# Last rope group's parts in buffers of their own, made and moved eight tiles later; VectorE casts tiles 3, 5 and 7 of a batch

## What is computed

```python
c_kv = x @ w_dkv
c_q = x @ w_dq
k_r = _apply_rope((x @ w_kr).reshape(b, s, 1, DR), cos, sin)
k_n = (c_kv @ w_uk).reshape(b, s, HKV, DN)
q_r = _apply_rope((c_q @ w_qr).reshape(b, s, H, DR), cos, sin)
q_n = (c_q @ w_uq).reshape(b, s, H, DN)
q = jnp.concatenate([q_r, q_n], axis=-1)
v = (c_kv @ w_uv).reshape(b, s, HKV, DV)
scores = jnp.einsum('bqhd,bkhd->bhqk', q, k) * scale
attn = jax.nn.softmax(scores, axis=-1)
out = jnp.einsum('bhqk,bkhd->bqhd', attn, v)
```

## Time and profile before

| | |
|---|---|
| median of 3 runs | 903.22 us (901.86 to 906.53) |
| the profiled execution | 900.48 us, its span 898.7 us |
| TensorE matmul, busy share | 96% |
| ScalarE | 76% |
| VectorE | 75% |
| GpSimd | 69% |

### The profile page before, as it was taken

How to read it: one execution, slowest core, us unless ns; L and a number is a source line. 1 busy time by engine, 2 the same in 40 slices (tenths; PEclk the granted TensorE clock), 3 DMA queues, 4 the chain that set the end, 5 groups by cost and what they waited for, 6 DMA issues and landing times.

```text
span 898.7 us, 16917 instructions
## 1 busy us (share of the span) xinstructions
PE 860.2 (96%) x5128; PEld 498.8 (56%) x5128; DVE 675.0 (75%) x1063; ACT 682.0 (76%) x1111; POOL 616.5 (69%) x438
## 2 busy tenths in 40 slices
PE   8999789999999999999999978999999999999995
PEld 5568344445444454458786733445444454446874
DVE  1879987888888888863577987888888888884455
ACT  2744789999999999971453489999999999995142
POOL 0318867888878888881344786788878887786135
PEclk8999999999999999999999999999999999999998
DMA  9865999999898899996201699999899999998101
GB/s 243 236 241 119 181 205 176 173 196 173 162 193 169 169 186 174 168 179 217 94 24 36 153 191 194 179 178 191 163 175 187 169 171 191 172 174 181 61 1 48
DMA packets 423964, 145.82 MB, mean 162 GB/s; under 512 B 408220, under 2 KB 416240, under 8 KB 423152
## 3 DMA queue, kind: packets, MB, share of 16 engines
q1 hardware_dynamic: 423152, 142.91, 78.2%
q0 software_dynamic: 608, 2.10, 0.7%
q10 hardware_dynamic: 160, 0.26, 0.1%
HBM read 23.85 MB, written 7.60 MB: 35 GB/s over the span
## 4 chain that ended last, share of the span: by engine, by line
PE 71%; DVE 8%; SPq 5%; ACT 4%; POOL 4%; issue 4%; DMA 4%; DVEq 0%; ACTq 0%; POOLq 0%
PE Tb L1269 18%; PE OO L1240 13%; PE Sa L1240 12%; PE Sb L1240 8%; PE Ta L1251 5%; PE Sa L1387 3%; PE Sb L1387 2%; SPq L369 2%; SPq L338 2%; DMA PT_dma<-P_parts 1%; PE Sb L1279 1%; ACT probs L633 1%; POOL turned L442 1%; DVE QO L1023 1%; PE OO L1129 1%
## 5 line engine op out<-in xcount | busy, mean ns | idle before, releaser
L468 POOL TENSOR_TENSOR P_parts<-probs,P_parts 128x768 f16<-128x768 f32 x256 | 419.9, 1658 | 106.5 <-ACT P_parts L526 106.4
L526 ACT ACTIVATE P_parts<-probs 128x768 f16<-128x768 f32 x256 | 205.6, 842 | 6.5 <-DMA PT_dma<-P_parts 5.2
L926 DVE TENSOR_TENSOR PT_lo<-Ta,PT_hi 128x512 f16<-128x512 f32 x128 | 88.5, 691 | 62.5 <-ACT PT_hi L526 60.0
L902 DVE TENSOR_REDUCE small<-OO 128x1 f32<-128x1024 f32 x96 | 117.1, 1220 | 21.4 <-PE OO L1240 21.4
L1269 PE MATMUL Tb<-PT_dma,V_hi 128*64 128x512 f16 x768 | 132.1, 385 | 0.0
L633 ACT ACTIVATE probs<-OO,small,scales 128x1024 f32<-128x1024 f32 x96 | 115.4, 1202 | 18.3 <-DVE small L905 16.7
L1240 PE MATMUL OO<-K_hi,Q_parts 128*128 128x512 f16 x384 | 115.5, 383 | 10.1 <-ACT probs L633 8.3
L902 DVE TENSOR_REDUCE small<-Sa 128x1 f32<-128x1024 f32 x96 | 116.9, 1217 | 8.4 <-PE Sa L1240 8.4
L1240 PE MATMUL Sa<-K_hi,Q_parts 128*128 128x512 f16 x384 | 115.9, 384 | 3.6 <-ACT probs L633 3.6
L633 ACT ACTIVATE probs<-Sa,small,scales 128x1024 f32<-128x1024 f32 x96 | 115.6, 1204 | 4.9 <-DVE small L905 2.5
L902 DVE TENSOR_REDUCE small<-Sb 128x1 f32<-128x1024 f32 x64 | 77.9, 1218 | 12.1 <-PE Sb L1240 12.1
(11 more groups left out here) (303 smaller groups left out, 1551.7 us busy)
## 6 DMA issues: line engine op xcount, KB each, us to landing
Q_parts<-turned_parts SPq DMA_DIRECT2D x64, 128.0 KB, 2.4
TT<-ternary SPq DMA_DIRECT2D x2, 2304.0 KB, 8.4
Q_parts<-Q_parts SPq DMA_DIRECT2D x16, 256.0 KB, 3.1
PT_dma<-P_parts SPq DMA_TRANSPOSE x256, 3.9
ternary<-tern SPq DMA_DIRECT2D x1, 2304.0 KB, 9.9
wo<-in_L_attn_w_o_dram SPq DMA_DIRECT2D x4, 512.0 KB, 9.7
xq<-in_L_attn_x_dram SPq DMA_DIRECT2D x2, 1024.0 KB, 10.6
wq_low<-Wq_lo SPq DMA_DIRECT2D x1, 2048.0 KB, 14.3
```

Of the source, the lines that this page charges most:

```text
L468: nc.gpsimd.tensor_tensor(P_parts[:, n % DEEP, 1, :], probs[n % DEEP][:, KP * P:S], P_parts[:, n % DEEP, 0, :], ALU.subtract).then_inc(par ...
L526: return nc.scalar.activation(o, i, ACT.Copy, scale=scale)
L902: nc.vector.tensor_reduce(nmax[:, n % 4:n % 4 + 1], scores_bank(n)[:, :], AX.X, ALU.max, negate=True).then_inc(row_max, 1)
L926: nc.vector.tensor_tensor(PT_lo[place].rearrange("p k (t q) -> p t k q", t=2), T_BANK[:, :].rearrange("p (t k q) -> p t k q", t=2, k=KP), ...
```

## The change

- The rotated halves of group 3 go to a buffer `turned_end` and their parts to `parts_end`. Both lie where `Wq_lo` was. So GpSimd's two sums of group 3 now wait until all query products are done (`q_ps`), and no longer for the low parts of group 2.
- VectorE makes the parts of group 3 in the steps n = 8 and n = 12 of pair 0, not in n = 0 and n = 2.
- SyncE issues group 3's latent moves ahead of tiles 9 and 10, and its rotary moves ahead of tiles 13 and 15. Before it prefetches `Wvo_lo` and `xr` (which lie where the new buffers are) it waits for those moves.
- The 768-column cast of tiles 3, 5 and 7 of each batch is done by VectorE (`odd_high`), directly behind `PT_lo`. GpSimd then waits for `odd_hi`.
- TensorE's wait for group 3 stands at the end of each of the pairs 1 to 6, not of pair 0.

```diff
+ODD = (3, 5, 7)
...
+        (turned_end, parts_end), AT = lay(
+            K_AT - H * 2 * P * 4, ("turned_end", [P, 2, S], F), ("parts_end", [P, 2, 2, S], F16))
...
-                        if first and n in (3, 5):
+                        if first and n == 8:
+                            for j in range(2):
+                                sp.wait_ge(turned_out[j], (b + 1) * 64 * GROUPS - 64)
+                        if first and n in (9, 10):
+                            t = 4 * (GROUPS - 1) + 2 * (n - 9)
+                            sp.wait_ge(lat_lo, (b + 1) * 4 * GROUPS)
+                            sp.dma_start(Q_parts[64:128, t, :, :], Q_parts[0:64, t + 1, :, :]).then_inc(lat_moved, 16)
+                        if first and n in (13, 15):
                             sp.wait_ge(lat_moved, (b + 1) * 32 * GROUPS)
-                            rotary_moves(GROUPS - 1, n // 2 - 1)
-                        if first and n == 8:
-                            sp.wait_ge(lat_moved, (b + 1) * 32 * GROUPS)
-                            for j in range(2):
-                                sp.wait_ge(turned_out[j], (b + 1) * 64 * GROUPS)
+                            rotary_moves(GROUPS - 1, n // 2 - 6)
...
+                for j in range(2):
+                    sp.wait_ge(turned_out[j], (b + 1) * 64 * GROUPS)
...
-                        if g >= 1:
+                        if g == GROUPS - 1:
+                            pool.wait_ge(q_ps, (b + 1) * 4 * GROUPS)
+                        elif g >= 1:
                             pool.wait_ge(rope_lo[j], b * GROUPS + g)
...
+                    if odd:
+                        pool.wait_ge(odd_hi, b * len(ODD) + ODD.index(n) + 1)
+                        pool.sem_inc(part_hi, 1)
+                    else:
+                        hold(pool, part_hi, tile + 1)
...
+                            if not (first and n + 3 in ODD):
+                                cast(n + 3)
...
+                def odd_high(tile, n):
+                    dve.wait_ge(exp_done, EXP0 + tile + 1)
+                    if n >= DEEP:
+                        dve.wait_ge(part_in[n % DEEP], 16 * (tile // DEEP))
+                    nc.vector.tensor_copy(P_parts[:, n % DEEP, 0, :], probs[n % DEEP][:, KP * P:S]).then_inc(odd_hi, 1)
...
-                        if first and n in (0, 2):
-                            rotary_parts_high(GROUPS - 1, n // 2)
+                        if first and n in (8, 12):
+                            rotary_parts_high(GROUPS - 1, n // 4 - 2)
                         transposed_low(pair * (TILES // 2) + n // 2, n + 1)
-                        if first and n in (0, 2):
-                            rotary_parts_low(GROUPS - 1, n // 2)
+                        if first and n in (8, 12):
+                            last_parts_low(n // 4 - 2)
+                        if first and n + 3 in ODD:
+                            odd_high(t0 + n + 3, n + 3)
...
-                        if first and n == TILES - 2:
+                        if not (first or last) and n == TILES - 2:
                             pe.wait_ge(lat_moved, b * 32 * GROUPS + 32 * GROUPS)
```

More of the change, by code:

```diff
@@ L96, in build @@
             K_AT - H * 2 * P * 4, ("Wvo_lo", [P, PAIRS, D], R), ("xr", [P, QT, D], F))
+        assert AT <= K_AT
+        (turned_end, parts_end), AT = lay(
+            K_AT - H * 2 * P * 4, ("turned_end", [P, 2, S], F), ("parts_end", [P, 2, 2, S], F16))
         assert AT <= K_AT
@@ L243, in build @@
         pt_ps, pt_hi, pt_lo = sem("pt_ps"), sem("pt_hi"), sem("pt_lo")
-        part_hi, part_lo = sem("part_hi"), sem("part_lo")
+        part_hi, part_lo, odd_hi = sem("part_hi"), sem("part_lo"), sem("odd_hi")
         part_in = tuple(sem(f"part_in{i}") for i in range(DEEP))
@@ L335, in rotary_moves @@
                 def rotary_moves(g, j):
+                    parts = parts_end if g == GROUPS - 1 else turned_parts
                     sp.wait_ge(rope_lo[j], b * GROUPS + g + 1)
@@ L338, in rotary_moves @@
                         sp.dma_start(Q_parts[32 * j:32 * j + 32, 4 * g + s, :, :],
-                                     turned_parts[32 * s:32 * s + 32, j, :, :]).then_inc(turned_out[j], 16)
+                                     parts[32 * s:32 * s + 32, j, :, :]).then_inc(turned_out[j], 16)
                 for g in range(GROUPS):
@@ L345, in _ @@
                         t = 4 * g + 2 * i
-                        sp.wait_ge(lat_lo, b * 4 * GROUPS + 4 * g + 2 * i + 2)
-                        sp.dma_start(Q_parts[64:128, t, :, :], Q_parts[0:64, t + 1, :, :]).then_inc(lat_moved, 16)
+                        if g < GROUPS - 1:
+                            sp.wait_ge(lat_lo, b * 4 * GROUPS + 4 * g + 2 * i + 2)
+                            sp.dma_start(Q_parts[64:128, t, :, :], Q_parts[0:64, t + 1, :, :]).then_inc(lat_moved, 16)
                     if g < GROUPS - 1:
@@ L463, in low_out, with low_probs @@
                                             O_parts[:, pair_row, cols].bitcast(F), ALU.subtract).then_inc(out_lo, 1)
-                def low_probs(tile, n):
-                    hold(pool, part_hi, tile + 1)
+                def low_probs(tile, n, odd=False):
+                    if odd:
[3 more added lines that the diff above has]
+                        hold(pool, part_hi, tile + 1)
                     nc.gpsimd.tensor_tensor(P_parts[:, n % DEEP, 1, :], probs[n % DEEP][:, KP * P:S],
@@ L474, in pair_pool @@
                         h = n // 8
-                        low_probs(pair * TILES + n, n)
+                        low_probs(pair * TILES + n, n, first and n in ODD)
                         if n % 8 == 0 and not (first and h == 0):
@@ L681, in pair_act @@
                         if ahead and behind:
-                            cast(n + 3)
+                            if not (first and n + 3 in ODD):
+                                cast(n + 3)
                 part_high(b * PAIRS * TILES, 0, None)
@@ L918, in rotary_parts_high, with last_parts_low @@
                     dve.wait_ge(rope_sum, b * 2 * GROUPS + 2 * g + j + 1)
-                    dve.wait_ge(turned_out[j], b * 64 * GROUPS + 64 * g)
-                    nc.vector.tensor_copy(turned_parts[:, j, 0, :], turned[:, j, :]).then_inc(rope_hi, 1)
+                    nc.vector.tensor_copy(parts_end[:, j, 0, :], turned_end[:, j, :]).then_inc(rope_hi, 1)
+                def last_parts_low(j):
+                    dve.wait_ge(rope_hi, (b + 1) * 2 * GROUPS - 1 + j)
+                    nc.vector.tensor_tensor(parts_end[:, j, 1, :], turned_end[:, j, :], parts_end[:, j, 0, :],
+                                            ALU.subtract).then_inc(rope_lo[j], 1)
                 def transposed_low(tile2, n):
```

3 lines of the change are left out of this document (2 added, 1 removed).

## The result

The changed kernel takes 910.09 us (median of 12 runs, 907.14 to 913.4), the kernel before 902.73 us (median of 12 runs beside it). The ratio is 1.0088 (95% interval 1.0071 to 1.0105): slower by about 0.9%. The forecast of 904.8, its range to 908.2 and its likeliest case, no measurable change, were all wrong. The two medians differ by 7.4 us, where 1.6 were forecast.

What follows compares the result with a forecast made beforehand. TensorE was taken to bound settled attention, a VectorE-ScalarE chain the first half of pair 0. Losses of 1.2 us (batch 1) and 0.4 (batch 0), +1.6 on the median 903.22, gave 904.8 us; range 898.8 to 908.2.

Steps and rivals of the forecast that it cites:

- The chain without group 3: First half of pair 0: VectorE-ScalarE chain of 4.43 us a step, tile 9's exponential 2.4 us earlier in batch 1.
- The piece in n = 8: Pair 0, one half of group 3's parts on VectorE: step of 6.83 us, leaving 0.4 of the 2.4 us gained.
- The piece in n = 12: Pair 0, other half of group 3's parts: step of 7.2 us, tile 17's exponential 1.9 us late in batch 1.
- VectorE's share: Pair 0, TensorE's loss after both pieces: 1.2 us in batch 1 and 0.4 in batch 0, +1.6 us.
- The sum's term for SyncE: End of pair 0: later moves delay tile 16's DMA 4 us, tile 20's cast waits; counted 0, bound 1 us a batch.
- Rival 2: TensorE's clock falls after idling before tile 15: 1.6 us lost a batch, 908.0 us in all; chance 0.11.
- Rival 3: VectorE's new casts of tiles 5 and 7 each wait 1.1 us for GpSimd: 909.2 us in all; chance 0.07.
- Rival 1: Group 3's pieces in n = 8 and 12 miss GpSimd, each step costing 1.9 us: 898.4 us in all; chance 0.25.
- TensorE's wait in the loop: Hardware loop: wait finds its counts already reached; counted 0, with 1.8 us as the bound over 12 loop turns.
- GpSimd's later wait: GpSimd's sums of group 3 wait for `q_ps`: at most 0.2 us, hidden.
- The 0.70 for no measurable change: Whole kernel: chance 0.70 that the time stays within what a measurement can tell, about 0.5% or 4.5 us.

Runs made afterwards that it cites:

- relief3_fill: Changed kernel with both remedies, relief3's SyncE order and fill's extra transposes on idle TensorE: ratio 1.0005, 0.5 us over the kernel before.
- relief3: Changed kernel, SyncE's second four rotary moves behind tile 15's DMA, first prefetch in the middle of pair 1: ratio 1.0034, 3.1 us over the kernel before.
- no_vector_parts: Changed kernel without VectorE's casts and subtractions of group 3; the rotary moves stay and carry group 2's parts: ratio 1.0107, 9.6 us over the kernel before.
- fill: Changed kernel with extra transposes on idle TensorE ahead of the scores of tiles 7 and 15: ratio 1.0051, 4.6 us over the kernel before.
- casts_only: Kernel before with only the casts of tiles 3, 5 and 7 put on VectorE: ratio 0.9989, 1.0 us under the kernel before.
- sync_relief: Changed kernel, SyncE's second four rotary moves behind tile 15's DMA, first prefetch behind pair 1: ratio 1.0055, 5.0 us over the kernel before.

## Why the prediction was wrong, step by step

- **The chain without group 3: right.** 4.37 us a step (forecast 4.43), the cast 0.55 (0.53), e(7) at 8.8 to 9.9 (8.8). From e(7) to e(9) I had 5.1; it is 4.46 at the full clock and 4.8 to 5.7 with the fall.
- **The piece in n = 8: right.** 6.82 us for the step (6.83), with the cast at 1.77 and the subtraction at 2.41. TensorE was idle for 2.36 us before tile 15's scores (forecast about 2.4).
- **The piece in n = 12: right.** 6.9 us (7.2). At the full clock e(17) comes at 35.96, 0.8 us later than before in batch 1 and level in batch 0. I had 1.9 and 1.1. So VectorE's share, 1.6 us in the sum, was if anything too large: relief3_fill shows 0.5 (-1.4 to 2.2).
- **The sum's term for SyncE: this failed.** I counted 0, with 1 us a batch as the bound, and relief3 shows 4.8 us for the two batches. I took the landing times of the earlier trace rows and asked only whether tile 16's DMA is met. I had 4 us as its delay. It was 5.2 in batch 1 (42.9 us behind e(3) instead of 37.7), since SyncE waits first for VectorE's late subtraction and then for the moves to land. This DMA then took 6.5 us to land, more than the 6.0 of the earlier trace rows, and the cast of tile 20 waited 2.62 us. And I did not ask how much room the queue has at a tile's pace of 2.3 us. no_vector_parts shows that: 3.5 us of SyncE's time a tile from tile 9 to 15, and 9.6 us over the kernel before with no piece on VectorE. A part of the 9.6 is half clock behind idle times of 5.89 and 4.53 us.
- **The clock: the rival was named, its place and its chance were wrong.** Rival 2 had the fall ahead of tile 15, 1.6 us a batch, at 0.11. fill shows 3.3 us for the two batches, close to its 3.2, but by two places and not one, so that agreement is luck. I missed the other place: I wrote that the idle time of the first half goes away, and 2.48 us of it stay. There the half clock was hidden before; with the chain shortened it is on the path. A cover that the change itself removes was counted as still there.
- **Rival 3** (the new casts meet GpSimd): didn't happen. All 72 of these casts in the twelve traces with them took 0.55, and casts_only shows no loss. **Rival 1** didn't happen either: in the changed kernel three of the four VectorE instructions of group 3 in batch 1 took longer beside GpSimd's (1.77, 2.41 and 2.22 us).
- **TensorE's wait in the loop and GpSimd's later wait**: nothing, as counted.

The two missed terms, 4.8 and 3.3, with the 0.5 of the pieces make 8.6 us. Measured were 7.9; the 0.7 between them is less than the runs can tell. The 0.70 for no measurable change rested on the sum and failed with it.

## What to carry over

When work is moved to a place where the bound engine runs without gaps, every queue that carries it needs its own sum there: how long it is busy for one tile, against the time of one tile. Here SyncE's transfers had room in the slow first steps and next to none afterwards, and taking VectorE's work away only changed who waited. And when a chain gets shorter, ask again what it used to hide; here it was TensorE's half clock.

## What the runs showed of the hardware

The same idle time of TensorE was followed by a fall of its clock in one place and not in another. These are all its idle times of at least 1.3 us from 6 us ahead of e(3) to the seam in the 14 traces:

| idle before the matmul | clock fell to 0.50 within 3 us | stayed at 1.00 |
|---|---|---|
| 1.45 to 2.10 us | 0 | 9 |
| 2.36 to 2.37 us (tile 15) | 5 | 3 |
| 2.48 to 2.56 us (tile 7) | 10 | 7 |
| 3.02 us and more | 10 | 1 |

The same place in the same kernel goes either way: in the changed kernel's trace the 2.36 us ahead of tile 15 were followed by a fall in batch 1 and not in batch 0. After 2.48 us ahead of tile 7 it fell in both batches; here, in sync_relief, after the same 2.48 us, it did not:

```profile
108.50 0.60 PE L1274 MATMUL OO<-K_hi,Q_parts 128*128 128x512 f16 x2 [2.48 <-ACT probs L654]
```

```profile
109.00:110.00 1.00, 1.00 (x7) 0.53 (x6) 1.00 (x2) 1.00 (x2) 0.15 (x1) 1.00 1.11 225
110.00:111.00 1.00, 1.00 (x8) 0.63 (x7) 1.00 (x2) 0.96 (x3) 0.69 (x1) 1.00 1.11 199
```

The Trainium skill, TensorE: Matmul & The Clock Gate, Part 1: The HAM clock gate, says of the rise to the full clock that its place varies from run to run of the same kernel. The table shows the like for the fall, which that sentence does not speak of.

The mean granted clock of each run goes with its time. Of the changed kernel's twelve runs the three at 0.990 or 0.991 took 907.14 to 909.31 us, and the five above 911 us had 0.980 to 0.984. So falls of the clock probably make a part of the spread of 6.3 us from fastest to slowest; no run separates that from the rest.

Left open: whether SyncE's own time in its instructions or the DMA engines behind it are the tighter limit. Both are nearly full in these stretches, and no run takes one of them apart from the other.
